# One scale for gate and up, and a new order for the end of the first attention block, in a one-core language-model block

## Chip, core and metric

The kernel runs on one core of one Trainium2 chip. The metric is the device time of one execution in microseconds (us); lower is better. The core's engines are named as in the profile: PE (TensorE: matmuls, with its weight loads as PEld), DVE (VectorE), ACT (ScalarE), POOL (GpSimd) and SP (SyncE, which here only issues DMAs).

## What is computed

The reference takes token ids of shape (2, 1024) with 128 possible values, and gives 2048 rows of 512 numbers. Cut to what matters:

```python
h = rms_norm(rms_norm(emb[x], norm_weight) @ proj.T)            # 2048 rows of 512
a = layernorm(h)
q, k, v = a @ wq, a @ wk, a @ wv      # 32 query heads, 8 key/value heads, 16 wide
y = causal_softmax(q @ k.T / 4) @ v   # each key/value head serves 4 query heads
h = h + y @ wo
b = layernorm(h)
return h + (silu(b @ w_gate.T) * (b @ w_up.T)) @ w_down.T       # hidden width 2048
```

Since h before the attention depends on the token alone, the kernel builds tables over the 128 tokens, and works on rows fetched from them.

## The kernel before

**Blocks and slots.** The 2048 rows are 16 tiles of 128 (`t`), two tiles to a block (`n`, 0 to 7). `phase(n, att, ffn, m)` is called on each engine for n = 0 to 8. It interleaves the attention of block n with the feed-forward part of block m = n - 1 in 24 slots (`s`). Phase 0 has attention alone, and is the stage that the change touches most; the last phase has the feed-forward part alone. The order on each engine is the order in which the code is written, slot by slot, with the places of single steps in tables of slot numbers (`FIRST_SLOTS` for phase 0, `HI_FIRST`, `LOW_FIRST`, `GRAM`, `FILL`). Nothing reorders it. Engines wait for each other by semaphores.

**Attention.** A block has 16 units (`V`), one for a tile and a key/value head. Of unit V = 16n + s, slot s holds on PE `score(V)` and `turn(V+1)` (a transpose of the next queries), on ACT the copy `stack` and the exponential (L516), and on DVE the multiplication with the counts (L835), whose semaphore is `w_rdy`. PE's `values(V)` follows two slots later in phases 0 and 1. After each pair of units DVE takes a reciprocal (L842) and writes a part of `y` (L845); the eighth pair of phase 0 ends the block's attention.

**End of a tile.** For each tile the slot tables place a chain of steps: `yt` (PE transposes y, L1140; ACT copies it as f16 high half, L550; DVE makes the low half, L863), `wo` (PE, 12 products of 512 columns: high by high, high by low and low by high for four chunks, L1148 to L1150), `ln` (DVE: the sum `h1`, L871, and its statistics, L873 to L875), `rs` (DVE: a reciprocal root in eight small dependent steps, L586 to L590), `xhat` (DVE, L881), `xn` (PE transposes, L1155; ACT high half, L559) and `xl` (DVE low half, L885). `tail(t)` is the PSUM bank that these steps share: bank 0 for tile 0, bank 7 for all others. In the text, yt(1) is that step of tile 1.

**Weights of the feed-forward part.** Gate, up and down come as f32 in 24 chunks of 1024 columns, and each is split into an f16 high half by ACT (`split_high`, L482 and L483) and a low half by DVE (`split_low`, L774 and L776). In chunks 0 to 15 the first 512 columns are gate and the others up, each with a scale of its own. The scales come from Gram products, 128 of 128x128 for gate and up (`gate_up_gram`) and 64 for down (L1174, table `GRAM`): DVE takes the diagonals (L738, L739), PE sums them over partitions (L1132), DVE takes the maximum and makes powers of two (`weight_scales`). Chunks 0 to 3 are split in phase 0 and the others in phase 1, one a slot. PE's filler products (L1168, table `FILL`) write results that nobody reads.

**Feed-forward.** `gate_up(m, s)` makes one hidden chunk of 128 in 24 products of 256 columns (L1112 to L1114): gate and up, four chunks each, by high-high, high-low and low-high. The first call, `gate_up(0, 0)`, stands at the head of phase 1. Its wait is

```python
if s == 0:
    pe.wait_ge(xt_lo, m * TPB + TPB)
```

which asks for the low halves of both tiles of the block.

## Time and profile before

| | |
|---|---|
| median of 3 runs | 723.21 us (722.03 to 723.68) |
| profiled execution, its own time | 722.6 us |
| its span, first to last instruction | 720.9 us |
| granted TensorE clock, mean | 0.985 of full speed |
| busy: PE, DVE, ACT, POOL | 693.6, 413.4, 334.1, 295.6 us |
| matmuls | 6399 |

The span is 1.7 us shorter than the execution's own time. The tables over the tokens take the first 45 us, phase 0 runs from there to about 92.8 us, and phase 1 begins with the first gate product at 92.8 us.

### The profile page before, as it was taken

To read this page: it belongs to the slowest core of one execution; us is meant where nothing else is said; L and a number is where in the kernel's file an instruction comes from. 1 tells how busy PE (TensorE), PEld (TensorE's weight loads), DVE (VectorE), ACT (ScalarE), POOL (GpSimd) and SP (SyncE) were. 2 spreads that over 40 slices of the span, in tenths; PEclk is the share of its full clock that TensorE was granted. 3 is DMA by queue.
4 is the path that set the end of the run, shared out by engine and by line. 5 is a ranking of instruction groups with operands and counts; after the bars stand their busy time and mean duration, and the time that the engine had idled before them with its cause. 6 is when DMAs were issued, how large, how long until landed. Compare 5 with 4: busy or idle time off the path is not lost.

```text
span 720.9 us, 16337 instructions
## 1 busy us (share of the span) xinstructions
PE 693.6 (96%) x6399; PEld 530.9 (74%) x6399; DVE 413.4 (57%) x1038; ACT 334.1 (46%) x692; POOL 295.6 (41%) x398
## 2 busy tenths in 40 slices
PE   8459999999999999999999999999999999999998
PEld 5359679974898569965997489856996499847873
DVE  7767789885654456554655465455655365543320
ACT  6426378762565226631665046522674066512320
POOL 5020212241365426752565436642665246611220
PEclk9859999999999999999999999999999999999999
DMA  8759400011000110002000210012000300000000
GB/s 314 307 199 409 145 38 1 2 30 61 33 2 1 61 62 2 2 20 96 7 2 2 70 53 3 1 47 75 2 2 1 107 15 2 1 16 15 2 1 29
DMA packets 10459, 40.37 MB, mean 56 GB/s; under 512 B 1808, under 2 KB 2576, under 8 KB 8592
## 3 DMA queue, kind: packets, MB, share of 16 engines
q1 hardware_dynamic: 6912, 25.44, 9.0%
q0 software_dynamic: 3328, 13.11, 5.8%
q8 instruction: 51, 0.84, 0.5%
q10 hardware_dynamic: 144, 0.79, 0.3%
q14 instruction: 24, 0.20, 0.1%
HBM read 29.89 MB, written 9.44 MB: 55 GB/s over the span
## 4 chain that ended last, share of the span: by engine, by line
PE 89%; DVE 7%; ACT 2%; issue 1%; POOL 1%; DVEq 0%; ACTq 0%; POOLq 0%
PE banks L1112 15%; PE banks L1113 15%; PE banks L1114 15%; PE banks L1203 6%; PE banks L1205 6%; PE banks L1204 6%; PE banks L1066 4%; PE banks L1084 3%; PE banks L1055 2%; PE banks L1148 2%; PE banks L1149 2%; PE banks L1150 2%; PE banks L1046 1%; PE banks L1090 1%; PE banks L1091 1%
## 5 line engine op out<-in xcount | busy, mean ns | idle before, releaser
L1114 PE MATMUL banks<-xnT_and_h,ffn_weights 128*128 128x256 f16 x1024 | 279.0, 272 | 0.0
L1113 PE MATMUL banks<-xnT_and_h,ffn_weights 128*128 128x256 f16 x1024 | 278.9, 272 | 0.0
L1112 PE MATMUL banks<-xnT_and_h,ffn_weights 128*128 128x256 f16 x1024 | 278.8, 272 | 0.1
L375 POOL TENSOR_TENSOR gated_split<-gate_work,gated_split 128x256 f16<-128x256 f32 x128 | 86.7, 677 | 260.6 <-ACT gated_split L520 260.6
L379 POOL TENSOR_TENSOR weights_split<-weights,weights_split 128x512 f16<-128x512 f32 x96 | 111.3, 1160 | 0.0
L1112 PEld LDWEIGHTS banks<-xnT_and_h,ffn_weights 128*128 128x128 f16 x1024 | 101.0, 99 | 11.8 <-DVE xnT_and_h L885 0.6
L1114 PEld LDWEIGHTS banks<-xnT_and_h,ffn_weights 128*128 128x128 f16 x1024 | 100.0, 98 | 11.7
L1113 PEld LDWEIGHTS banks<-xnT_and_h,ffn_weights 128*128 128x128 f16 x1024 | 100.0, 98 | 11.3
L508 ACT ACTIVATE gate_work<-banks,scales 128x256 f32<-128x256 f32 x128 | 60.6, 474 | 99.8 <-PE banks L1114 99.6
L835 DVE SCALAR_TENSOR_TENSOR weights<-weights,counts_T 128x512 f32<-128x512 f32 x128 | 87.8, 686 | 10.9 <-ACT weights L516 10.8
L516 ACT ACTIVATE weights<-banks,scales 128x512 f32<-128x512 f32 x128 | 87.3, 682 | 14.5 <-PE banks L1066 14.5
L801 DVE COPY q_stack<-banks 128x256 f16<-128x256 f16 x96 | 27.8, 290 | 102.8 <-PE banks L1055 102.8
L823 DVE SCALAR_TENSOR_TENSOR gate_work<-gate_work,banks 128x256 f32<-128x256 f32 x128 | 52.9, 414 | 58.9 <-ACT gate_work L508 58.6
L1205 PE MATMUL banks<-ffn_weights,gated_split 128*128 128x512 f16 x224 | 84.9, 379 | 0.0
L1204 PE MATMUL banks<-ffn_weights,gated_split 128*128 128x512 f16 x224 | 84.9, 379 | 0.0
L1203 PE MATMUL banks<-ffn_weights,gated_split 128*128 128x512 f16 x224 | 84.8, 379 | 0.0
L520 ACT ACTIVATE gated_split<-gate_work 128x256 f16<-128x256 f32 x128 | 53.4, 417 | 67.5 <-DVE gate_work L828 67.5
L526 ACT ACTIVATE weights_split<-weights 128x512 f16<-128x512 f32 x96 | 58.9, 614 | 0.0
L828 DVE SCALAR_TENSOR_TENSOR gate_work<-banks,gate_work 128x256 f32<-128x256 f32 x128 | 54.3, 424 | 4.4
L331 POOL DMA_INDIRECT token_rows<-token_table,indices x16 | 15.7, 983 | 92.5 <-DVE xnT_and_h L871 86.9
L559 ACT ACTIVATE xnT_and_h<-banks 128x512 f16<-128x512 f32 x16 | 9.6, 597 | 81.0 <-PE banks L1155 80.5
L1066 PE MATMUL banks<-q_stack,k_stack_even 128*128 128x128 f16 x256 | 42.7, 220 | 1.0 <-ACT q_stack L491 1.0
(241 smaller groups left out, 1065.1 us busy)
## 6 DMA issues: line engine op xcount, KB each, us to landing
ffn_weights<-in_ffn_w SPq DMA_DIRECT2D x12, 1024.0 KB, 10.2
out_rows_dram<-ffn_weights SPq DMA_DIRECT2D x16, 256.0 KB, 2.0
xnT_and_h<-in_wqkv SPq DMA_DIRECT2D x1, 1536.0 KB, 8.9
local_table<-gated_split SPq DMA_DIRECT2D x2, 640.0 KB, 4.5
local_table<-xnT_and_h SPq DMA_DIRECT2D x2, 640.0 KB, 5.7
gated_split<-in_projT SPq DMA_DIRECT2D x4, 256.0 KB, 4.4
ffn_weights<-in_wo SPq DMA_DIRECT2D x1, 1024.0 KB, 10.9
token_table<-weights_split ACTq DMA_DIRECT2D x1, 768.0 KB, 5.6
```

Source lines behind the costliest of these rows:

```text
L375: g.tensor_tensor(gtl[:, j, :], g2[j % 2], gth[:, j, :], ALU.subtract).then_inc(gt_lo, 1)
L379: g.tensor_tensor(WTl[V % RING], E[V % RING][:, :], WTh[V % RING], ALU.subtract).then_inc(wt_lo, 1)
L508: a.activation(th[j % 2], f_bank[j % 3][:, 0:BLK], ACT.Tanh, scale=c_tanh).then_inc(th_rdy, 1)
L516: a.activation(E[V % RING][:, :], b_S[V % 2], ACT.Exp, scale=c_exp).then_inc(exp_done, 1)
L835: v.scalar_tensor_tensor(w, w, SEEN_MAX, cT[:, t * P:(t + 1) * P].unsqueeze(1).broadcast_to([P, REP, P]), ALU.min, ALU.mult).then_inc(w_rd ...
L1066: last = t.matmul(b_S[V % 2][:, (2 * j + a) * P:(2 * j + a + 1) * P], (KstA, KstB)[a][:, gr * P:(gr + 1) * P], Qst[:, r * 256 + j * P:r * ...
L1112: t.matmul(o, wh, xTh[m % 2][:, c, :], start=c == 0, stop=False)
L1113: t.matmul(o, wh, xTl[m % 2][:, c, :], start=False, stop=False)
L1114: last = t.matmul(o, wl, xTh[m % 2][:, c, :], start=False, stop=c == DC - 1)
L1203: t.matmul(o, hh, dn_w(j, 0), start=j == 0, stop=False)
L1204: t.matmul(o, hh, dn_w(j, 1), start=False, stop=False)
L1205: last = t.matmul(o, hl, dn_w(j, 0), start=False, stop=j == HC - 1)
```

## The change

Gate and up get one common scale: the Gram products of both accumulate in one bank, one diagonal is taken and summed, and each chunk is split by one operation of 1024 columns on ACT and one on DVE. Chunks 0 to 3 are split in other slots of phase 0. The down Gram products, 64 in four slots from 16 on, become 64 in three slots from 17 on, behind the last `values`. `wo` takes its high halves first and waits for the low half of y ahead of the last four products only; for tile 1 it writes bank 4 (`b_S[0]`). `h1` gets a slot entry of its own, ahead of `ln`. The copy that signalled `y_rdy` in phase 0 (L849) goes, and yt waits on `pv_ev`. In all gate and up chunks the four high-by-low-activation products of gate, and of up, stand behind the other eight, and the first gate product of a block waits for the high halves of both tiles and the low half of the first. The diff, cut to its core:

```diff
-FIRST_SLOTS = dict(yt=(11, 18), wo=(13, 19), ln=(16, 20), rs=(17, 20), xhat=(19, 20), xn=(20, 21), xl=(21, 21), ...
+FIRST_SLOTS = dict(yt=(11, 18), wo=(13, 19), h1=(16, 20), ln=(17, 20), rs=(19, 20), xhat=(19, 20), xn=(20, 21), xl=(21, 21), ...
-HI_FIRST = {16: 0, 17: 1, 20: 2, 21: 3}
-LOW_FIRST = {19: (0,), 21: (1,), 22: (2,), 23: (3,)}
+HI_FIRST = {13: 0, 16: 1, 17: 2, 21: 3}
+LOW_FIRST = {13: (0,), 21: (1,), 22: (2,), 23: (3,)}
-GRAM = {16: (0, 12), 17: (12, 24), 18: (24, 44), 19: (44, 64)}
+GRAM = {17: (0, 18), 18: (18, 34), 19: (34, 64)}
...
+        def wo_bank(t):
+            return b_S[0] if t == 1 else tail(t)
...
-                a.activation(half(i, 0)[:, 0:512], raw(i)[:, 0:512], ACT.Copy, scale=s_g if i < 16 else s_d)
-                a.activation(half(i, 0)[:, 512:1024], raw(i)[:, 512:1024], ACT.Copy,
-                             scale=s_u if i < 16 else s_d).then_inc(split_hi, 1)
+                a.activation(half(i, 0), raw(i), ACT.Copy, scale=s_gu if i < 16 else s_d).then_inc(split_hi, 1)
...
-                v.tensor_tensor(t_gu_diag[:, 0:P], f_bank[2][:, 0:P], ident[:, :], ALU.mult)
-                v.tensor_tensor(t_gu_diag[:, P:2 * P], b_tail[:, 0:P], ident[:, :], ALU.mult).then_inc(tab["gu_diag"], 1)
+                v.tensor_tensor(t_gu_diag, f_bank[2][:, 0:P], ident[:, :], ALU.mult).then_inc(tab["gu_diag"], 1)
...
-                        if i == 3:
-                            dve.wait_ge(pv_ev, pair + 1)
-                            v.tensor_scalar(st[:, 25:26], rden[k][:, 0:1], 1.0, None, ALU.mult).then_inc(y_rdy, 1)
...
             def gate_up(m, s):
                 i = m * HC + s
                 if s == 0:
-                    pe.wait_ge(xt_lo, m * TPB + TPB)
+                    pe.wait_ge(xt_hi, m * TPB + TPB)
+                    pe.wait_ge(xt_lo, m * TPB + 1)
...
                     for c in range(DC):
                         wh, wl = (gu_w(s, up, c, h) for h in (0, 1))
                         t.matmul(o, wh, xTh[m % 2][:, c, :], start=c == 0, stop=False)
-                        t.matmul(o, wh, xTl[m % 2][:, c, :], start=False, stop=False)
-                        last = t.matmul(o, wl, xTh[m % 2][:, c, :], start=False, stop=c == DC - 1)
+                        t.matmul(o, wl, xTh[m % 2][:, c, :], start=False, stop=False)
+                    if s == 0 and up == 0:
+                        pe.wait_ge(xt_lo, m * TPB + TPB)
+                    for c in range(DC):
+                        last = t.matmul(o, gu_w(s, up, c, 0), xTl[m % 2][:, c, :], start=False, stop=c == DC - 1)
...
                         if att and s == at["wo"][k]:
-                            pe.wait_ge(yt_lo, tl + 1)
+                            if tl == 1:
+                                pe.wait_ge(yt_hi, tl + 1)
+                            else:
+                                pe.wait_ge(yt_lo, tl + 1)
```

**PE, slots 16 to 19 of phase 0.** In the kernel before, `ffn_weights` rows are the down Gram products, the `v_full_one` rows are values(14) and values(15), and L1140 is yt(1); the first `wo_split` row opens wo(1):

```order
L1084 MATMUL banks<-v_full_one,weights 128x17 [waits w_ready,pv_evacuated]
L1084 MATMUL banks<-v_full_one,weights 128x17 x3
L1174 MATMUL banks<-ffn_weights 128x128 [waits ffn_pair8_in]
L1174 MATMUL banks<-ffn_weights 128x128 x11
L1084 MATMUL banks<-v_full_one,weights 128x17 [waits w_ready]
L1084 MATMUL banks<-v_full_one,weights 128x17 x3
...
L1140 MATMUL banks<-ident,xnT_and_h 128x128 [waits y_ready]
L1140 MATMUL banks<-ident,xnT_and_h 128x128 x3
...
L1148 MATMUL banks<-wo_split,yT_split 128x512 [waits yT_lo]
```

The same place in the changed kernel, where L1082 is `values`, L1186 the down Gram products, L1145 yt(1), and L1156, L1157 and L1162 are wo(1):

```order
L1082 MATMUL banks<-v_full_one,weights 128x17 [waits w_ready,pv_evacuated]
L1082 MATMUL banks<-v_full_one,weights 128x17 x3
L1082 MATMUL banks<-v_full_one,weights 128x17 [waits w_ready]
L1082 MATMUL banks<-v_full_one,weights 128x17 x3
L1186 MATMUL banks<-ffn_weights 128x128 [waits ffn_pair8_in]
...
L1145 MATMUL banks<-ident,xnT_and_h 128x128 [waits pv_evacuated]
L1145 MATMUL banks<-ident,xnT_and_h 128x128 x3
...
L1156 MATMUL banks<-wo_split,yT_split 128x512 [waits yT_hi]
...
L1162 MATMUL banks<-wo_split,yT_split 128x512 [waits yT_lo]
```

values(15) now stands directly behind values(14), ahead of all Gram products. Between it and yt(1) stand 18 of them where there were 12, between yt(1) and wo(1) 16 where there were 20, and behind wo(1) 30 where there were 20. wo(1) waits for the high half of y first.

**DVE, slots 16 to 20 of phase 0.** In the kernel before, from h1(0) to h1(1) (both L871), with the pair of the last values (L842, L845), the eight steps of rs(0) (L586 to L590, of which two stand here), yt(1)'s low half (L863), xhat(0) (L881) and the split of chunk 0 (L774, L776):

```order
L875 TENSOR_SCALAR ln_stats<-ln_stats 128x1 [waits vector_step]
L842 RECIPROCAL rden<-banks 128x8 [waits pv_ready,vector_step]
L845 TENSOR_TENSOR xnT_and_h<-banks,rden 128x128 [waits rden_ready]
L849 TENSOR_SCALAR ln_stats<-rden 128x1 [waits pv_evacuated]
L586 TENSOR_SCALAR ln_stats<-ln_stats 128x1
L587 TENSOR_SCALAR ln_stats<-ln_stats 128x1 [waits vector_step]
...
L863 TENSOR_TENSOR yT_split<-banks,yT_split 128x512 [waits yT_hi,vector_step]
L881 TENSOR_SCALAR xn<-xnT_and_h,ln_stats 128x512
L774 SCALAR_TENSOR_TENSOR ffn_weights<-ffn_weights,scales 128x512 [waits split_hi]
L776 SCALAR_TENSOR_TENSOR ffn_weights<-ffn_weights,scales 128x512
L871 SCALAR_TENSOR_TENSOR xnT_and_h<-banks,scales,token_rows 128x512 [waits wo_ready]
```

In the changed kernel, from the pair of the last values (L841, L844) to h1(1) (L868), with the low half of y at L860:

```order
L841 RECIPROCAL rden<-banks 128x8 [waits pv_ready]
L844 TENSOR_TENSOR xnT_and_h<-banks,rden 128x128 [waits rden_ready]
L871 BN_STATS ln_stats<-xnT_and_h 128x6 [waits h1_ready]
L872 BN_AGGR ln_stats<-ln_stats 128x2 [waits vector_step]
L873 TENSOR_SCALAR ln_stats<-ln_stats 128x1 [waits vector_step]
L860 TENSOR_TENSOR yT_split<-banks,yT_split 128x512 [waits yT_hi,vector_step]
L591 TENSOR_SCALAR ln_stats<-ln_stats 128x1
...
L879 TENSOR_SCALAR xn<-xnT_and_h,ln_stats 128x512 [waits vector_step]
L868 SCALAR_TENSOR_TENSOR xnT_and_h<-banks,scales,token_rows 128x512 [waits wo_ready]
```

The last pair moved ahead of tile 0's statistics, the low half of y ahead of rs(0), and the split of chunk 0 out of this stretch.

**DVE, slots 13 to 15.** In the changed kernel the split of chunk 0 (L777) stands behind the scale (L751) and ahead of the multiplications of units 14 and 15 (L834), for which values(14) and values(15) wait; ACT's half of it stands likewise ahead of the stack and the exponentials of these units:

```order
L750 TENSOR_SCALAR scales<-scales 128x1
L751 TENSOR_SCALAR scales<-scales 128x1
L777 SCALAR_TENSOR_TENSOR ffn_weights<-ffn_weights,scales 128x1024 [waits split_hi,tab_gu_scaled]
L834 SCALAR_TENSOR_TENSOR weights<-weights,counts_T 128x512 [waits exp_done] x2
L841 RECIPROCAL rden<-banks 128x8 [waits pv_ready]
```

Before, nothing stood between the scale and the two multiplications.

## Rows read from the trace of the kernel before

**Rows 1.** The page's chain that ended last, shares of the span by engine:

```profile
PE 89%; DVE 7%; ACT 2%; issue 1%; POOL 1%; DVEq 0%; ACTq 0%; POOLq 0%
```

**Rows 2.** Busy us (x count) of PE, PEld, DVE, ACT, POOL; granted clock; DMA:

```profile
100.00:160.00 60.00, 60.00 (x571) 53.42 (x569) 54.30 (x99) 46.17 (x99) 17.71 (x25) 1.00 0.01 2
```

**Rows 3.** Timeline of PE: start, us, operation, idle before it:

```profile
71.32 0.70 PE L1132 MATMUL banks<-gate_work,xnT_and_h 128*128 128x256 f32 x2
...
77.60 0.96 PE L1084 MATMUL banks<-v_full_one,weights 128*128 128x17 f32 x8
...
79.09 1.01 PE L1084 MATMUL banks<-v_full_one,weights 128*128 128x17 f32 x8
79.95 0.85 PE L1174 MATMUL banks<-ffn_weights 128*128 128x128 bf16 x12
81.35 0.66 PE L1140 MATMUL banks<-ident,xnT_and_h 128*128 128x128 f32 x4 [0.54 <-DVE ln_stats L849]
...
83.68 0.39 PE L1148 MATMUL banks<-wo_split,yT_split 128*128 128x512 f16 x1 [0.53 <-DVE yT_split L863]
...
86.28 1.31 PE L1174 MATMUL banks<-ffn_weights 128*128 128x128 bf16 x20
...
90.73 0.66 PE L1155 MATMUL banks<-ident,xn 128*128 128x128 f32 x4 [0.97 <-DVE xn L881]
91.22 0.39 PE L1165 MATMUL banks<-gate_work,xnT_and_h 128*128 128x128 f32 x2
91.44 1.24 PE L1168 MATMUL banks<-counts_T,ident 128*128 128x512 f16 x5
92.80 0.28 PE L1112 MATMUL banks<-xnT_and_h,ffn_weights 128*128 128x256 f16 x1
...
93.03 0.27 PE L1114 MATMUL banks<-xnT_and_h,ffn_weights 128*128 128x256 f16 x1
```

**Rows 4.** Timeline of DVE:

```profile
70.98 0.28 DVE L739 TENSOR_TENSOR gate_work<-banks,ident 128x128 f32<-128x128 f32 x1
...
74.03 0.20 DVE L747 TENSOR_SCALAR scales<-scales 128x1 f32<-128x1 f32 x1
...
77.22 0.69 DVE L835 SCALAR_TENSOR_TENSOR weights<-weights,counts_T 128x512 f32<-128x512 f32 x1 [0.48 <-ACT weights L516]
...
80.57 0.21 DVE L842 RECIPROCAL rden<-banks 128x8 f32<-128x8 f32 x1 [0.40 <-DVE ln_stats L875]
...
81.21 0.14 DVE L586 TENSOR_SCALAR ln_stats<-ln_stats 128x1 int32<-128x1 int32 x1
...
82.93 0.69 DVE L863 TENSOR_TENSOR yT_split<-banks,yT_split 128x512 f16<-128x512 f32 x1
83.54 0.54 DVE L881 TENSOR_SCALAR xn<-xnT_and_h,ln_stats 128x512 f32<-128x512 f32 x1
83.99 0.74 DVE L774 SCALAR_TENSOR_TENSOR ffn_weights<-ffn_weights,scales 128x512 f16<-128x512 f32 x1
...
86.48 0.75 DVE L871 SCALAR_TENSOR_TENSOR xnT_and_h<-banks,scales,token_rows 128x512 f32<-128x512 f32 x1 [1.08 <-PE banks L1150]
...
92.05 0.69 DVE L885 SCALAR_TENSOR_TENSOR xnT_and_h<-banks,xnT_and_h 128x512 f16<-128x512 f32 x1 [0.58 <-ACT xnT_and_h L559]
```

**Rows 5.** Timeline of ACT:

```profile
75.26 0.68 ACT L516 ACTIVATE weights<-banks,scales 128x512 f32<-128x512 f32 x1
...
82.12 0.60 ACT L550 ACTIVATE yT_split<-banks 128x512 f16<-128x512 f32 x1 [2.48 <-PE banks L1140]
```

**Rows 6.** One line's instructions each: duration ns min/median/max, first and last start:

```profile
L472 ACT ACTIVATE wo_split<-ffn_weights,scales x2: 1144/1148/1151, 50.9 to 52.8; 128x1024 f16<-128x1024 f32 x2
...
L733 DVE SCALAR_TENSOR_TENSOR wo_split<-ffn_weights,scales,wo_split x2: 1279/1280/1280, 59.1 to 66.9; 128x1024 f16<-128x1024 f32 x2
...
L774 DVE SCALAR_TENSOR_TENSOR ffn_weights<-ffn_weights,scales x16: 741/1118/1235, 84.0 to 141.0; 128x512 f16<-128x512 f32 x16
```

**Rows 7.** The page's costliest groups: busy, mean ns | idle before:

```profile
L1114 PE MATMUL banks<-xnT_and_h,ffn_weights 128*128 128x256 f16 x1024 | 279.0, 272 | 0.0
```

More of the change, by code:

```diff
@@ L238, in col @@
             return sc[:, i:i + n]
-        s_q, s_k, s_v, s_wo, s_g, s_u, s_d = (col(8 + i) for i in range(7))
+        s_q, s_k, s_v, s_wo, s_gu, s_d = (col(8 + i) for i in range(6))
         r_q, r_k, r_v = (col(16 + i) for i in range(3))
@@ L863, in phase @@
                             v.tensor_tensor(yT[:, D:2 * D], tail(t), yT[:, 0:D], ALU.subtract).then_inc(yt_lo, 1)
-                        if att and s == at["ln"][k]:
+                        if att and s == at["h1"][k]:
                             dve.wait_ge(wo_rdy, t + 1)
@@ L870, in phase @@
                                 dve.wait_ge(fin_rdy, t - 3)
-                            v.scalar_tensor_tensor(h1[t % 4], tail(t), c_vo, h0g[k], ALU.mult, ALU.add).then_inc(h1_rdy, 1)
+                            v.scalar_tensor_tensor(h1[t % 4], wo_bank(t), c_vo, h0g[k], ALU.mult, ALU.add).then_inc(h1_rdy, 1)
+                        if att and s == at["ln"][k]:
                             dve.wait_ge(h1_rdy, t + 1)
@@ L894, in phase @@
                         stack((n + 1) * UPB)
+                    if n == 0 and s == GU_SCALE_SLOT:
+                        weight_scales()
                     if n == 0:
@@ L903, in phase @@
                         place_max(1)
-                    if n == 0 and s == GU_SCALE_SLOT:
-                        weight_scales()
                     if n == 0 and s == WO_SCALE_SLOT:
@@ L1045, in gate_up_gram @@
                     w = raw_pair(i).bitcast(BF16)[:, o:o + 2 * P - 1:2]
-                    last = t.matmul((f_bank[2], b_tail)[m][:, 0:P], w, w, start=u == 8 * m, stop=u == 112 + 8 * m + 7)
+                    last = t.matmul(f_bank[2][:, 0:P], w, w, start=u == 0, stop=u == 127)
                 return last
@@ L1131, in phase @@
                         pe.wait_ge(tab["gu_diag"], 1)
-                        t.matmul(b_tail[:, P:3 * P], ones32, t_gu_diag, start=True, stop=True).then_inc(tab["gu_sum"], 1)
+                        t.matmul(b_tail[:, P:2 * P], ones32, t_gu_diag, start=True, stop=True).then_inc(tab["gu_sum"], 1)
                     for k in range(TPB):
@@ L1146, in phase @@
                             for c in range(DC):
-                                yh, yl = (yT[:, i * D + c * P:i * D + (c + 1) * P] for i in (0, 1))
-                                t.matmul(tail(tl), yh, Woh[:, c, :], start=c == 0, stop=False)
-                                t.matmul(tail(tl), yh, Wol[:, c, :], start=False, stop=False)
-                                last = t.matmul(tail(tl), yl, Woh[:, c, :], start=False, stop=c == DC - 1)
+                                yh = yT[:, c * P:(c + 1) * P]
+                                t.matmul(wo_bank(tl), yh, Woh[:, c, :], start=c == 0, stop=False)
+                                t.matmul(wo_bank(tl), yh, Wol[:, c, :], start=False, stop=False)
+                            if tl == 1:
+                                pe.wait_ge(yt_lo, tl + 1)
+                            for c in range(DC):
+                                yl = yT[:, D + c * P:D + (c + 1) * P]
+                                last = t.matmul(wo_bank(tl), yl, Woh[:, c, :], start=False, stop=c == DC - 1)
                             last.then_inc(wo_rdy, 1)
```

38 lines of the change are left out of this document (20 added, 18 removed).

## Prediction

> **What bounds the kernel now.** I read the chain of waits first. PE holds 89% of it and DVE 7% [rows 1], so time can be won only where PE waits, or where it does work that nobody needs. The view by stretches says where that is: from 100 to 160 us PE is busy for 60.00 of 60 us at a granted clock of 1.00 [rows 2]. So from phase 1 on a start that comes earlier should move everything behind it by as much. What is left is the end of phase 0, and there I read the timelines of PE, DVE and ACT beside each other.
>
> The chain there runs as follows. values(15) starts at 79.09 us on PE and its pair is taken up by DVE at 80.57 [rows 3, 4]. PE meanwhile does 12 Gram products, and then idles 0.54 us until yt(1) at 81.35 [rows 3]. DVE does the eight steps of rs(0) from 81.21 to 82.93, and only then the low half of y, though ACT's high half, started at 82.12 and 0.60 long, was done at 82.72 [rows 4, 5]. wo(1) waits for that and starts at 83.68 [rows 3]. h1(1) starts at 86.48 [rows 4]. From there a fixed chain on DVE (statistics, root, xhat) leads to the transposes xn(1) at 90.73, ACT's high half and DVE's low half, which starts at 92.05 and takes 0.69, and the first gate product at 92.80 [rows 3, 4]. DVE's split of chunk 0, at 83.99 [rows 4], stands in this stretch but ahead of a wait for PE, which costs h1(1) nothing.
>
> **The change, part by part.** I lay the changed order out with the durations of the rows.
>
> *Scale of gate and up.* PE's sum at 71.32 [rows 3] waits for the second diagonal, which starts on DVE at 70.98 and is 0.28 long [rows 4]. Without it the sum starts between nothing and 0.28 earlier; I take 0.15. The sum over 256 columns runs 0.70 to its end, one over 128 columns 0.39 (L1165) [rows 3]: 0.31 less. Together 0.46. wo(0) and all that PE has in order behind it can be that much earlier: values(14), which started at 77.60 without a wait [rows 3], could start at 77.14.
>
> *Split of chunk 0 in slot 13.* The last step of the scale starts at 74.03 [rows 4]; with a maximum over half the columns I put it at 73.9, and ACT starts at about 74.14. A split of 1024 columns takes 1.15 on ACT [rows 6]: until 75.29. Behind it on ACT wait the stack for score(15) and the exponential of unit 14, which started at 75.26 before [rows 5] and now at about 75.47, ending at 76.15. DVE starts its half of the split at 75.34 and is free 1.20 later (1.28 long, with the usual overlap of 0.08) [rows 6]: 76.54. Behind it waits the multiplication of unit 14, done now at 77.23, and that of unit 15, done at 77.84, as against 77.91 before (77.22 + 0.69) [rows 4]. So values(14) starts at 77.28, not at 77.14: it gains 0.32. Bounds: 0.46 if the wait is shorter, and nothing or a loss of 0.3 if the handovers between ACT and DVE take 0.3 to 0.6 more. I stay near the rows, since GpSimd is idle then: the split's longest times, 1235 ns as against 741 [rows 6], are from phase 1.
>
> *values(15) ahead of the Gram products.* It follows values(14) by 0.86 (79.09 to 79.95) [rows 3]: 78.14, 0.95 earlier. Of this 0.63 is the first Gram share, 12 products of 0.057 each (0.85 less a last one of 0.22, over 11) [rows 3].
>
> The Trainium skill ("TensorE: Matmul & The Clock Gate", Back-to-back issue gap) gives about 81 ns for each product of 128 columns in a stream with its weight loads, where the row has 57. By its figure, an estimate, the 18 and 16 products that now stand before and behind yt(1) would take 0.8 us more than by the row, of which about 0.6 would reach the chain. The row is of these very products, and I keep to it.
>
> *yt(1).* DVE took up the pair 1.48 after values(15) started (80.57 - 79.09) and yt(1) started 0.78 later; I take 0.19 off for the copy L849, since small DVE steps that wait for each other follow at about that (eight of them in the 1.72 of rs(0)) [rows 4]: 0.59. So yt(1) starts 2.07 after values(15): 80.21, and 18 Gram products (0.86 + 1.03 = 1.89) hide under this. It gains 1.14. Of the 1.48, 0.4 is idle time that I can't put to a cause; if it goes, the products bound it, and the gain is 0.18 more.
>
> *Low half of y, and wo(1).* Let Y be the start of yt(1). ACT's high half starts 0.77 after it (82.12 - 81.35), and ends at Y + 1.37 [rows 3, 5]. On PE the transposes (0.49) and 16 Gram products (0.92) end at Y + 1.41, so wo(1) starts at Y + 1.42. DVE now waits with the low half ahead of rs(0), so rs(0), xhat(0) and h1(1) are queued behind that wait; it ends at Y + 2.11, while PE has high products until Y + 3.15. wo(1) ends 2.60 after its start (83.68 to 86.28) [rows 3], and its signal takes 0.20: Y + 4.22. On DVE the low half holds the engine 0.61, rs(0) 1.72 (81.21 to 82.93) and xhat(0) 0.45 (83.54 to 83.99) [rows 4]: free at Y + 4.20. Both meet, and h1(1) starts at Y + 4.22, where it was Y + 5.13. It gains 0.91 more, together 2.05. The next thing late is DVE's own queue: nothing more is to be had here by a faster PE. Bank 4 for wo(1) costs nothing by itself, since DVE reads bank 7 meanwhile.
>
> *Down to the first gate product.* From h1(1) to xn(1) nothing changes (4.25). The 30 Gram products behind wo(1) take 1.7 and the 8 fillers 1.7, which end before xn(1) at 88.68. Then PE has 0.49 of transposes, 0.22, and five fillers, which end 1.08 after 91.44 before, that is 1.79 after xn(1). ACT's high half is done 1.3 after xn(1), just ahead of 92.05. So the fillers bound the first gate product, at 1.79 where the low half gave 2.07: 0.28 more. Tile 1's low half, done 2.0 after xn(1), is asked for only behind eight products of about 0.11 each (92.80 to 93.03 for two) [rows 3], at 2.67.
>
> *Everything else.* The merged splits in phase 1 save about 0.12 on DVE and 0.17 on ACT in each chunk, but PE waits for neither there [rows 2]: worth nothing. POOL's fetches hang on h1 and move with it. The sum is 0.32 + 0.63 + 0.19 + 0.91 + 0.28 = 2.33 us. The profiled execution took 722.6 by its own time, and should take 720.3; from the median of 723.21, which is 0.6 above it, I come to **720.9**.
>
> **The rivals.**
>
> *It gives less, 0 to 1.4 us (about 722.4).* The split of chunk 0 stands in slot 13 ahead of the last two units. Each us by which the multiplication of unit 14 is later than 77.23 is a us on values(14) and all behind. If ACT and DVE together take 0.9 more, through a collision as in phase 1 (up to 0.5 on one split [rows 6]) and longer handovers, the gain falls to 1.4. Against it: ACT's and DVE's times for exactly these shapes are in the rows, and POOL has no work then.
>
> The Trainium skill ("Perfetto Trace Analysis", Optimizing Scalar/DVE Operations) says that where these engines aren't saturated but hold up others, breaking instructions up may let work be done sooner. By that rule the merged operations would be the wrong way here. The trace speaks against it in this place, since both halves were signalled together before.
>
> *It gets slower (from 723.7 on).* All gate and up products change their order: 3072 of them, with a mean of 272 ns in each of the three lines, of which one is shown [rows 7]. If two products in a row on one moving operand, or weights that change each time, cost 1 ns more each, that is 3.1 us, and 723.21 - 2.3 + 3.1 = 724.0. From 0.76 ns on it takes the whole gain. Against it: the three kinds stand in three different neighbourhoods now (same weights as before, same moving operand, or neither), and their three rows agree within 0.2 us in 279 [rows 7]. It is the only part that touches the bound stage.
>
> *The gain is lost again.* If phase 1 were held by DVE or ACT with PE only seeming busy, an earlier start would be eaten up, and the time stay at 723. DVE is busy 54.30 of 60 us there, so it is near [rows 2]; but PE shows no gap, and DVE's load falls.
>
> **How the numbers follow.** The case of the sum, gain between 1.4 and 2.8, has 0.76: 720.4 to 721.8. More than that has 0.04. Less, 0 to 1.4, has 0.13, the lost gain counted in. Slower through the products' rate or something unseen has 0.07. The runs before spread by 1.7, so a median may be off by some tenths; that widens the range to 719.8 to 722.3. A change of 0.2%, 1.4 us, is about what can be told from none: faster by more 0.79, within it 0.14, slower 0.07.
>
> **What would show it.** values(14) at about 77.3 and values(15) at 78.1 directly behind it; yt(1) near 80.2; wo(1) near 81.6 with DVE's low half of y running under it; h1(1) near 84.4, directly behind xhat(0) on DVE; the first gate product near 90.5, right behind the fillers. From there the gate products must keep following at about 0.11, and PE without gaps. The prediction is wrong if the first gate product moved by 2.3 and the end didn't, if values(14) waits for DVE beyond 77.6, or if the mean of the gate products is no longer 272 ns.

## The result, and the profile after

The changed kernel takes 721.12 us (median of 20 runs, 720.29 to 722.72) and the kernel before, on the same chip, 722.89. One of its 20 runs was in a slower state, at 739.27; such runs count in no ratio here, nor in any median from here on, and without it the kernel before has 722.77. The ratio is 0.9979, 95% interval 0.9972 to 0.9986: faster by 0.21%. The profiled execution took 720.69 by its own time, with a span of 718.9 and a mean granted clock of 0.986. The page of the changed kernel (busy times, chain, gate and up products):

```profile
PE 693.0 (96%) x6399; PEld 530.6 (74%) x6399; DVE 409.4 (57%) x1019; ACT 329.7 (46%) x668; POOL 297.1 (41%) x398
...
PE 89%; DVE 6%; ACT 2%; issue 1%; POOL 1%; DVEq 0%; ACTq 0%; POOLq 0%
...
L1112 PE MATMUL banks<-xnT_and_h,ffn_weights 128*128 128x256 f16 x1024 | 237.3, 272 | 0.0
L1111 PE MATMUL banks<-xnT_and_h,ffn_weights 128*128 128x256 f16 x1024 | 237.2, 272 | 0.0
...
L1116 PE MATMUL banks<-xnT_and_h,ffn_weights 128*128 128x256 f16 x1024 | 153.6, 273 | 0.0
```

The chain is PE's as before [rows 1], with 6% instead of 7% for DVE. The three lines of gate and up products have means of 272, 272 and 273 ns where the row of before had 272 [rows 7]; their busy sums can't be compared, since the view joins products that follow each other on one line. From 100 to 160 us PE is full, as before [rows 2], and DVE is down from 54.30 to 51.84 us:

```profile
100.00:160.00 60.00, 60.00 (x561) 52.64 (x559) 51.84 (x92) 42.76 (x81) 20.89 (x25) 1.00 0.04 11
```

The timeline of PE at the end of phase 0 (start, us, operation, idle before), which answers to [rows 3]:

```profile
70.90 0.49 PE L1134 MATMUL banks<-gate_work,xnT_and_h 128*128 128x128 f32 x2
71.22 0.38 PE L1156 MATMUL banks<-wo_split,yT_split 128*128 128x512 f16 x1
...
77.19 1.93 PE L1082 MATMUL banks<-v_full_one,weights 128*128 128x17 f32 x16
78.97 1.20 PE L1186 MATMUL banks<-ffn_weights 128*128 128x128 bf16 x18
80.00 0.60 PE L1145 MATMUL banks<-ident,xnT_and_h 128*128 128x128 f32 x4
80.44 1.08 PE L1186 MATMUL banks<-ffn_weights 128*128 128x128 bf16 x16
81.72 0.39 PE L1156 MATMUL banks<-wo_split,yT_split 128*128 128x512 f16 x1 [0.20 <-ACT yT_split L555]
...
84.32 1.88 PE L1186 MATMUL banks<-ffn_weights 128*128 128x128 bf16 x30
...
88.79 0.66 PE L1167 MATMUL banks<-ident,xn 128*128 128x128 f32 x4 [0.42 <-DVE xn L879]
...
89.51 1.24 PE L1180 MATMUL banks<-counts_T,ident 128*128 128x512 f16 x5
90.58 0.27 PE L1111 MATMUL banks<-xnT_and_h,ffn_weights 128*128 128x256 f16 x1
90.69 0.27 PE L1112 MATMUL banks<-xnT_and_h,ffn_weights 128*128 128x256 f16 x1
```

The same stretch on DVE, which answers to [rows 4]:

```profile
75.15 1.28 DVE L777 SCALAR_TENSOR_TENSOR ffn_weights<-ffn_weights,scales 128x1024 f16<-128x1024 f32 x1 [1.35 <-ACT ffn_weights L488]
76.36 1.29 DVE L834 SCALAR_TENSOR_TENSOR weights<-weights,counts_T 128x512 f32<-128x512 f32 x2
...
79.15 0.21 DVE L841 RECIPROCAL rden<-banks 128x8 f32<-128x8 f32 x1 [0.39 <-PE banks L1082]
...
81.77 0.69 DVE L860 TENSOR_TENSOR yT_split<-banks,yT_split 128x512 f16<-128x512 f32 x1 [1.07 <-ACT yT_split L555]
...
84.09 0.55 DVE L879 TENSOR_SCALAR xn<-xnT_and_h,ln_stats 128x512 f32<-128x512 f32 x1
84.55 0.75 DVE L868 SCALAR_TENSOR_TENSOR xnT_and_h<-banks,scales,token_rows 128x512 f32<-128x512 f32 x1
...
90.11 0.69 DVE L883 SCALAR_TENSOR_TENSOR xnT_and_h<-banks,xnT_and_h 128x512 f16<-128x512 f32 x1 [0.58 <-ACT xnT_and_h L564]
```

And on ACT [rows 5]:

```profile
73.89 1.15 ACT L488 ACTIVATE ffn_weights<-ffn_weights,scales 128x1024 f16<-128x1024 f32 x1 [2.78 <-DVE scales L751]
...
81.07 0.60 ACT L555 ACTIVATE yT_split<-banks 128x512 f16<-128x512 f32 x1 [2.44 <-PE banks L1145]
```

The first gate product is at 90.58 where it was at 92.80. But executions differ by up to 1.7 us in the time at which they reach phase 0's second half, and they do so for one and the same kernel too (69.95 and 71.25). So I measure from values(11), ahead of wo(0): at 70.18 before, 69.95 here, and at 69.8 to 71.5 over all profiles of this study. In the eight profiles in which PE is busy throughout from 49 to 55 us it goes with the granted clock there: 69.95 at 0.86, down to 71.52 at 0.71. The other six have 0.82 to 1.00 there and idle for 0.04 to 0.93 us, and are as late as 71.25, so the clock alone doesn't account for it. From values(11) to each step:

| us after values(11) | before | forecast | changed |
|---|---|---|---|
| values(14) | 7.42 | 7.10 | 7.24 |
| yt(1) | 11.17 | 10.03 | 10.05 |
| wo(1) | 13.50 | 11.4 | 11.77 |
| h1(1) | 16.30 | 14.25 | 14.60 |
| xn(1) | 20.55 | 18.50 | 18.84 |
| first gate product | 22.62 | 20.29 | 20.63 |
| from there to the end of the span | 628.1 | 628.1 | 628.3 |

The stretch is 1.99 shorter, values(11) was 0.23 earlier by chance, and 0.2 is given back behind the first gate product: together the 2.0 between the spans of 720.9 and 718.9.

### The profile page after: what moved, and what is told of

It is laid out like the page before. It is cut to its first block, busy times and chain, and to the rows that moved or that the text cites. A ratio compares the mean times of both kernels' runs of the same rounds, so it can differ in the third digit from the quotient of the medians.

```text
span 718.9 us, 16283 instructions
## 1 busy us (share of the span) xinstructions
PE 693.0 (96%) x6399; PEld 530.6 (74%) x6399; DVE 409.4 (57%) x1019; ACT 329.7 (46%) x668; POOL 297.1 (41%) x398
## 4 chain that ended last, share of the span: by engine, by line
PE 89%; DVE 6%; ACT 2%; issue 1%; POOL 1%; DVEq 0%; ACTq 0%; POOLq 0%
PE banks L1111 15%; PE banks L1116 15%; PE banks L1112 15%; PE banks L1215 6%; PE banks L1217 6%; PE banks L1216 6%; PE banks L1064 4%; PE banks L1082 4%; PE banks L1053 2%; PE banks L1156 2%; PE banks L1162 2%; PE banks L1157 2%; PE banks L1044 1%; PE banks L1088 1%; PE banks L1089 1%; PE banks L1145 1%
## 5 line engine op out<-in xcount | busy, mean ns | idle before, releaser
L1112 PE MATMUL banks<-xnT_and_h,ffn_weights 128*128 128x256 f16 x1024 | 237.3, 272 | 0.0
L1111 PE MATMUL banks<-xnT_and_h,ffn_weights 128*128 128x256 f16 x1024 | 237.2, 272 | 0.0
L1116 PE MATMUL banks<-xnT_and_h,ffn_weights 128*128 128x256 f16 x1024 | 153.6, 273 | 0.0
L1111 PEld LDWEIGHTS banks<-xnT_and_h,ffn_weights 128*128 128x128 f16 x1024 | 100.9, 99 | 11.4
L834 DVE SCALAR_TENSOR_TENSOR weights<-weights,counts_T 128x512 f32<-128x512 f32 x128 | 87.5, 684 | 9.1 <-ACT weights L520 8.8
```

The costliest lines, as they stand in the source:

```text
L834: v.scalar_tensor_tensor(w, w, SEEN_MAX, cT[:, t * P:(t + 1) * P].unsqueeze(1).broadcast_to([P, REP, P]), ALU.min, ALU.mult).then_inc(w_rd ...
L1111: t.matmul(o, wh, xTh[m % 2][:, c, :], start=c == 0, stop=False)
L1112: t.matmul(o, wl, xTh[m % 2][:, c, :], start=False, stop=False)
L1116: last = t.matmul(o, gu_w(s, up, c, 0), xTl[m % 2][:, c, :], start=False, stop=c == DC - 1)
```

## Experiments

The theory of the prediction was: each part shortens the stretch by its own wait, and nothing else moves. Its rivals were the split in slot 13, the rate of the reordered products, and an early start that phase 1 eats up. Of each kernel one execution was profiled. Where a step is given from values(11), its clock was 1.00 there unless the text says otherwise.

**The order of the products.** *u_gate* is the changed kernel with the products and the wait of the first gate product as before:

```diff
-                    pe.wait_ge(xt_hi, m * TPB + TPB)
-                    pe.wait_ge(xt_lo, m * TPB + 1)
+                    pe.wait_ge(xt_lo, m * TPB + TPB)
...
-                        t.matmul(o, wl, xTh[m % 2][:, c, :], start=False, stop=False)
...
+                        t.matmul(o, wh, xTl[m % 2][:, c, :], start=False, stop=False)
+                        last = t.matmul(o, wl, xTh[m % 2][:, c, :], start=False, stop=c == DC - 1)
```

> The changed kernel with the gate and up products in the order of before, and the first gate product waiting for both low halves again. Theory (the change works through the chain at the end of phase 0): the first gate product comes 0.28 us later after xn(1) (2.07 as before, 1.79 with the change), nothing else moves, so 0.3 us slower than the changed kernel and 1.2 to 1.5 faster than the kernel before. Rival (the order of the products changes PE's rate, and gave or took part of the gain in 3072 products): the time from the first gate product to the end of the span differs from the changed kernel's 628.3 us by over 0.5 us.

*gate_alone* makes only this edit, the other way round, on the kernel before.

> The kernel before with the new order of the gate and up products and the new waits of the first gate product alone. Theory: the first gate product starts 1.79 us after xn(1), where the low half made it 2.07: 0.28 us faster than before, 0.1 to 0.4 in the times. Rival (the order changes PE's rate): a difference of over 0.5 us either way, in the stretch behind the first gate product.

*u_gate* took 720.64 (ratio 0.9975, 0.9966 to 0.9985), *gate_alone* 722.76 (1.0001, 0.9992 to 1.0010). From the first gate product to the end, *gate_alone* needs 628.0 and *u_gate* 628.4, against 628.1 and 628.3 with the other order: 3072 reordered products cost 0.1 at most, and the rival that made it slower is ruled out. Timeline of PE in *gate_alone*:

```profile
90.77 0.66 PE L1159 MATMUL banks<-ident,xn 128*128 128x128 f32 x4 [0.97 <-DVE xn L881]
...
91.48 1.24 PE L1172 MATMUL banks<-counts_T,ident 128*128 128x512 f16 x5
92.56 0.27 PE L1113 MATMUL banks<-xnT_and_h,ffn_weights 128*128 128x256 f16 x1
```

The first gate product comes 1.79 after xn(1), behind the fillers, where it was 2.07: the 0.28 of the sum to the digit. It is too little to show in the times: *gate_alone* was no faster than the kernel before, and *u_gate*, forecast 0.3 slower than the changed kernel, has a median 0.5 lower, with intervals that overlap. *u_gate* has 2.07 again, yet its stretch, 20.50, is shorter than the changed kernel's 20.63. The reason is another step: ACT takes up yt(1) 0.64 after it starts (80.59 to 81.23), where the changed kernel's profile has 1.07. PE and ACT in *u_gate*:

```profile
80.59 0.60 PE L1141 MATMUL banks<-ident,xnT_and_h 128*128 128x128 f32 x4
```

```profile
81.23 0.60 ACT L555 ACTIVATE yT_split<-banks 128x512 f16<-128x512 f32 x1 [2.01 <-PE banks L1141]
```

With *u_gate*'s hand-over the changed kernel would stand at 20.50 - 0.28 = 20.22, and the next three, which have the short one too (0.64 to 0.69), are measured against that.

**The slots of the splits.** *u_slots* is the changed kernel with the splits where they were:

```diff
-HI_FIRST = {13: 0, 16: 1, 17: 2, 21: 3}
-LOW_FIRST = {13: (0,), 21: (1,), 22: (2,), 23: (3,)}
+HI_FIRST = {16: 0, 17: 1, 20: 2, 21: 3}
+LOW_FIRST = {19: (0,), 21: (1,), 22: (2,), 23: (3,)}
```

> The changed kernel with chunks 0 to 3 split in the slots of before (ACT in 16, 17, 20, 21, DVE in 19, 21, 22, 23). Theory (DVE's queue and PE's wo(1) reach h1(1) at the same time in the changed kernel): DVE's split of chunk 0, 1.20 us, now stands between xhat(0) and h1(1) and makes h1(1) 1.2 later, of which about 0.1 to 0.3 comes back because values(14) no longer waits for DVE; 0.9 to 1.1 us slower than the changed kernel, so 0.4 to 1.0 faster than before. Rival (DVE has slack there, only PE's order counts): no slower than the changed kernel, rather 0.2 faster.

It took 722.25 (0.9997, 0.9988 to 1.0006), and its stretch is 21.46. In the times nearly all of the gain is gone, where 0.4 to 1.0 had been expected to stay. By the stretch more stays: it is 1.16 shorter than before, and 0.95 is left with what is given back behind it. That lies just outside the interval, which ends at 0.87, and the runs don't show where the rest of the time goes. Timeline of its DVE:

```profile
84.20 0.55 DVE L879 TENSOR_SCALAR xn<-xnT_and_h,ln_stats 128x512 f32<-128x512 f32 x1
84.66 1.28 DVE L777 SCALAR_TENSOR_TENSOR ffn_weights<-ffn_weights,scales 128x1024 f16<-128x1024 f32 x1
85.86 0.74 DVE L868 SCALAR_TENSOR_TENSOR xnT_and_h<-banks,scales,token_rows 128x512 f32<-128x512 f32 x1
```

wo(1) had ended on PE at 84.13, but h1(1) stands behind the split of chunk 0 and starts at 85.86. The same split cost nothing before, since DVE waited 1.08 for PE there [rows 4]. Now h1(1) starts 5.68 after yt(1), where *u_gate* has 4.15: 1.53 more. Of this 0.29 comes back ahead of yt(1), which leaves the stretch 1.24 longer (21.46 - 20.22): values(14) comes 7.01 after values(11), against 7.24, so in slot 13 the split takes 0.23 from it.

**The place of the Gram products.** *u_gram* puts them back:

```diff
-GRAM = {17: (0, 18), 18: (18, 34), 19: (34, 64)}
+GRAM = {16: (0, 12), 17: (12, 24), 18: (24, 44), 19: (44, 64)}
```

> The changed kernel with the 64 down Gram products placed as before (12, 12, 20, 20 in slots 16 to 19). Theory: values(15) starts 0.69 us later behind 12 products, yt(1) 0.6 later, and the 20 products between yt(1) and wo(1) end 0.2 after ACT's high half, so the first gate product is 0.8 us later than in the changed kernel. Rival (the Gram products are hidden under the handovers to DVE and ACT): the first gate product moves by less than 0.3 us.

721.71 (0.9987, 0.9978 to 0.9996); the stretch 20.92. values(15) is 8.81 after values(11), yt(1) 10.45, which is 0.40 later than in the changed kernel. wo(1) comes 1.64 after yt(1), behind 20 Gram products where there were 16, and the stretch is 0.70 longer than 20.22.

**wo(1) by high halves first.** *u_wo* only makes wo(1) wait for the low half again:

```diff
                             if tl == 1:
-                                pe.wait_ge(yt_hi, tl + 1)
+                                pe.wait_ge(yt_lo, tl + 1)
```

> The changed kernel with wo(1) waiting for the low half of y ahead of its first product, the order of its products kept. Theory: wo(1) starts after DVE's low half, 0.7 us later, and h1(1) and the first gate product are 0.7 us later. Rival (DVE's queue in front of h1(1) is what counts, since it ends at the same time as wo(1)): under 0.2 us later.

721.41 (0.9985, 0.9976 to 0.9994). Timeline of its PE:

```profile
81.05 0.60 PE L1145 MATMUL banks<-ident,xnT_and_h 128*128 128x128 f32 x4
...
83.14 0.39 PE L1156 MATMUL banks<-wo_split,yT_split 128*128 128x512 f16 x1 [0.57 <-DVE yT_split L860]
```

wo(1) comes 2.09 after yt(1), against 1.36 in *u_gate* with the same hand-over, and the stretch is 20.98: 0.76 longer than 20.22. *wo_alone* brings the order of wo, bank 4 and the wait for the high half to the kernel before:

```diff
+                            if tl == 1:
+                                pe.wait_ge(yt_hi, tl + 1)
+                            else:
+                                pe.wait_ge(yt_lo, tl + 1)
...
-                                last = t.matmul(tail(tl), yl, Woh[:, c, :], start=False, stop=c == DC - 1)
...
+                            if tl == 1:
+                                pe.wait_ge(yt_lo, tl + 1)
+                            for c in range(DC):
+                                yl = yT[:, D + c * P:D + (c + 1) * P]
+                                last = t.matmul(wo_bank(tl), yl, Woh[:, c, :], start=False, stop=c == DC - 1)
```

> The kernel before with the new order of wo's products, wo(1) in bank 4 and waiting for the high half of y alone at its head. Theory: wo(1) starts 0.9 us earlier, at the end of ACT's high half, since the low half is late behind rs(0) on DVE and is there before it is asked for; h1(1) and the first gate product come 0.9 earlier, as DVE is done with its split of chunk 0 at 85.3 us: 0.6 to 1.0 faster than the kernel before. Rival (the three moves only pay together): under 0.3.

721.98 (0.9986, 0.9977 to 0.9995); stretch 21.92, 0.70 less than before. wo(1) starts 1.64 after yt(1), right behind 20 Gram products, and h1(1) 4.43 after it, where it was 5.13. It is the largest of the three parts that were made alone, and the only one of them that shows in the times.

**The common scale.** *scale_alone* is the kernel before with one scale, one diagonal and merged splits, in their old slots:

```diff
-                    last = t.matmul((f_bank[2], b_tail)[m][:, 0:P], w, w, start=u == 8 * m, stop=u == 112 + 8 * m + 7)
+                    last = t.matmul(f_bank[2][:, 0:P], w, w, start=u == 0, stop=u == 127)
...
-                v.tensor_tensor(t_gu_diag[:, P:2 * P], b_tail[:, 0:P], ident[:, :], ALU.mult).then_inc(tab["gu_diag"], 1)
```

> The kernel before with the common scale and the merged split operations alone, all slots as before. Theory: the sum over 128 columns and the one diagonal let wo(0) start about 0.5 us earlier on PE, and all up to values(14) with it, so the first gate product comes 0.4 to 0.5 us earlier; the merged splits give nothing, except where DVE's split of chunk 0 stands, under a wait for PE. Rival (the units behind it are held by ACT and DVE, not by PE's order): under 0.15 us; second rival (the merged splits relieve DVE in phase 1, which was the bound there): over 1 us, in the stretch behind the first gate product.

722.44 (0.9994, 0.9986 to 1.0003); stretch 22.12, 0.50 less. values(14) is at 7.01 and values(15) at 8.52, 0.39 earlier than before. The rest is in two hand-overs: DVE takes up the last pair 0.05 after it is free and values(15) has ended, where it took 0.40 before, which makes yt(1) another 0.22 earlier, and ACT is later behind yt(1), which takes 0.11 back. Nothing is given back behind the first gate product (628.0).

**Fewer fillers.** After the change the fillers bound the first gate product, which the kernels so far only inferred. *fill2* takes three of them away:

```diff
-FILL = {14: 2, 15: 2, 20: 8, 21: 5}
+FILL = {14: 2, 15: 2, 20: 8, 21: 2}
```

> The changed kernel with 2 fillers in slot 21 where there were 5. Theory: these fillers bound the first gate product, which then starts when ACT's high half is done, 1.32 us after xn(1) and not 1.79: 0.45 us faster than the changed kernel, 2.0 to 2.4 faster than before; the low half of tile 1 is in time behind eight products. Rival: the start is given back in phase 1, where chunk 1 to 3 and the next block's units wait for DVE, and the time stays; or the granted clock falls with less work on PE, and phase 1 gets slower by several us.

720.08 (0.9966, 0.9953 to 0.9979), stretch 20.24. The first gate product is at 90.99, 1.35 after xn(1) instead of 1.79, and now it is ACT that holds it, whose high half ends at 90.93 (timeline of ACT in *fill2*):

```profile
81.92 0.60 ACT L555 ACTIVATE yT_split<-banks 128x512 f16<-128x512 f32 x1 [2.50 <-PE banks L1145]
...
90.33 0.60 ACT L564 ACTIVATE xnT_and_h<-banks 128x512 f16<-128x512 f32 x1 [2.21 <-PE banks L1167]
```

**Three ways to have more.** *split_moved* is *fill2* with the splits in slots where they disturb neither values(14) nor h1(1):

```diff
-HI_FIRST = {13: 0, 16: 1, 17: 2, 21: 3}
-LOW_FIRST = {13: (0,), 21: (1,), 22: (2,), 23: (3,)}
+HI_FIRST = {15: 0, 16: 1, 20: 2, 21: 3}
+LOW_FIRST = {17: (0,), 21: (1,), 22: (2,), 23: (3,)}
```

> The kernel best with the fillers of slots 14 and 15 back (2 fillers in slot 21, chunk 0 split in ACT's slot 15 and DVE's slot 17). Theory (best lost its gain to the granted clock, 0.68 of full speed from 80 to 85 us, for want of those fillers): the clock stays at 1.00 there, values(14) starts behind PE's own order 0.2 us earlier than in the changed kernel, and the first gate product 20.0 us after values(11) as against 20.24 in fill2; 2.2 to 2.8 us faster than the kernel before. Rival (the clock falls because of the other 3 fillers or by chance): below 0.95 again in that stretch. Second rival: DVE's split in slot 17 makes the low half of y late, and the first gate product comes later than in fill2.

720.58 (0.9970, 0.9958 to 0.9981), stretch 20.29 where 20.0 was expected. values(14) is at 7.01, as it should be. But the timeline of DVE shows what takes the place of the wait:

```profile
80.53 1.28 DVE L777 SCALAR_TENSOR_TENSOR ffn_weights<-ffn_weights,scales 128x1024 f16<-128x1024 f32 x1 [0.30 <-DVE ln_stats L873]
81.73 0.68 DVE L860 TENSOR_TENSOR yT_split<-banks,yT_split 128x512 f16<-128x512 f32 x1
...
84.04 0.55 DVE L879 TENSOR_SCALAR xn<-xnT_and_h,ln_stats 128x512 f32<-128x512 f32 x1
84.50 0.75 DVE L868 SCALAR_TENSOR_TENSOR xnT_and_h<-banks,scales,token_rows 128x512 f32<-128x512 f32 x1
```

The split holds DVE until the low half of y at 81.73, 0.58 after ACT's high half ended (80.55 + 0.60); rs(0) and xhat(0) follow, and h1(1) starts at 84.50 although wo(1) had ended at 83.80, so that it is 3.30 behind the start of wo(1), against 2.79 in *u_gate*. What values(14) wins is lost in DVE's queue. *root_early* therefore has rs(0) in slot 18 and the low half of chunk 0 in slot 19:

```diff
-FIRST_SLOTS = dict(yt=(11, 18), wo=(13, 19), h1=(16, 20), ln=(17, 20), rs=(19, 20), xhat=(19, 20), ...
+FIRST_SLOTS = dict(yt=(11, 18), wo=(13, 19), h1=(16, 20), ln=(17, 20), rs=(18, 20), xhat=(19, 20), ...
...
-LOW_FIRST = {17: (0,), 21: (1,), 22: (2,), 23: (3,)}
+LOW_FIRST = {19: (0,), 21: (1,), 22: (2,), 23: (3,)}
```

> The kernel split_moved with rs(0) in slot 18, ahead of the low half of y, and DVE's split of chunk 0 in slot 19, behind xhat(0). In split_moved DVE was free for h1(1) 0.50 us after wo(1) and its signal were done. Theory: rs(0) fills DVE's wait for the high half of y, the low half comes just before wo(1) asks for it, xhat(0) and the split end 0.2 us after wo(1), and the first gate product comes 20.0 to 20.1 us after values(11) as against 20.29; 0.2 to 0.3 faster than split_moved, 2.2 to 2.9 faster than the kernel before. Rival: the low half of y comes too late behind rs(0), PE waits inside wo(1), and nothing is won.

720.60 (0.9965, 0.9951 to 0.9979), the same again. Its profiled execution, 721.67, lost clock (0.50 from 80 to 82 us), so its stretch of 21.08 can't be set against 20.29. In it h1(1) is 2.79 behind the start of wo(1) again, and DVE idles 0.96 ahead of it; but the low clock had made wo(1) late and so gave DVE time, and what the edit is worth at full clock stays open. *best*, made ahead of these two, has *split_moved*'s tables and leaves out the fillers of slots 14 and 15 too:

```diff
-FILL = {14: 2, 15: 2, 20: 8, 21: 2}
+FILL = {20: 8, 21: 2}
```

> The changed kernel with 2 fillers in slot 21, none in slots 14 and 15, and chunk 0 split behind the last exponential (ACT in slot 15, DVE in slot 17 behind tile 0's statistics, where it idles 1.07 us; ACT's chunk 2 back in slot 20). Theory: the last two units are held by nothing but their own chain, values(15) starts 0.9 to 1.1 us earlier than in the changed kernel, DVE's split hides in the wait for the high half of y, and with the fillers' 0.45 the first gate product comes 1.2 to 1.6 us earlier; 2.8 to 3.4 faster than before. Rival (the split in slot 13 costs nothing and the fillers hide under ACT's and DVE's handovers): only the 0.45 of fill2. Second rival: the granted clock falls with fewer fillers, and it is slower.

It took 721.28 (0.9979, 0.9970 to 0.9989), 1.4 less than before where 2.8 to 3.4 was expected: no better than the changed kernel, and 0.70 above *split_moved*, though the two intervals overlap. Its clock fell. Windows of *best* (us, busy and count of PE, PEld, DVE, ACT, POOL; granted clock; DMA):

```profile
78.00:80.00 2.00, 2.00 (x22) 2.00 (x22) 1.71 (x5) 1.76 (x2) 0.20 (x1) 0.94 0.06 16
80.00:82.00 2.00, 2.00 (x18) 2.00 (x17) 1.61 (x5) 0.00 (x0) 1.69 (x2) 0.50 0.36 55
82.00:84.00 2.00, 2.00 (x20) 1.72 (x20) 1.78 (x4) 0.60 (x1) 1.42 (x1) 0.71 0.85 334
```

The stretch is 20.44, 0.15 longer than in *split_moved*, although PE had four products less to do and ACT took up yt(1) as soon as it ended. All ten of its runs that count have a mean clock of 0.981 to 0.983, which no run of *split_moved* has (0.986 to 0.988). In the profile the fall takes what the missing fillers gave and 0.15 more; whether the rest of the 0.70 is real, and how it comes about, isn't shown.

**The changed kernel again.** *after_again* has no edit. It asks whether the hand-over to ACT, and this clock, belong to the kernel or to the execution.

> The changed kernel once more, unchanged. From the start of values(11) to the first gate product it had 20.63 us. In its first profile ACT took up the transposes of yt(1) 1.07 us after they started, in three of its variants 0.64, in one 1.13. Theory: this differs by execution and not by kernel, so that the stretch is 20.2 to 20.3 in an execution with 0.64, where the 16 Gram products bound wo(1), and 20.6 in one with 1.07. Rival: it belongs to the kernel, and is 1.07 again. Time against the kernel before: 0.9965 to 0.9985.

721.34 (0.9977, 0.9967 to 0.9987). Its profiled execution was its slowest, 723.15, and shows the clock of *best* without any edit (windows, columns as above):

```profile
78.00:80.00 2.00, 1.94 (x16) 1.54 (x14) 1.97 (x5) 1.93 (x2) 0.00 (x0) 1.00 0.04 14
80.00:82.00 2.00, 2.00 (x24) 2.00 (x24) 1.50 (x6) 0.00 (x0) 1.36 (x2) 0.70 0.12 23
82.00:84.00 2.00, 2.00 (x18) 1.93 (x17) 0.51 (x1) 0.60 (x1) 1.46 (x2) 0.50 0.89 270
84.00:86.00 2.00, 2.00 (x14) 1.05 (x12) 1.72 (x10) 0.00 (x0) 0.00 (x0) 0.94 0.32 121
```

In the changed kernel's first profile all these windows have 1.00. The stretch is 21.83 here, 1.2 longer. Its rows of yt(1) and of ACT's high half also bear on the other question, PE first:

```profile
81.70 1.05 PE L1145 MATMUL banks<-ident,xnT_and_h 128*128 128x128 f32 x4
```

```profile
82.79 0.60 ACT L555 ACTIVATE yT_split<-banks 128x512 f16<-128x512 f32 x1 [2.87 <-PE banks L1145]
```

ACT starts 1.09 after yt(1), as it did in the first profile (1.07). But the four transposes take 1.05 at this clock, not 0.60: ACT starts 0.04 after they end (82.75), where in the first profile it started 0.47 after (81.07 - 80.60). So by its end ACT took them up at once here. Since the transposes themselves were slow, this alone doesn't settle it: from their start the distance is the same as in the first profile. The stronger sign is in kernels whose programs are the changed kernel's up to this step: *u_gate* and *u_wo* have 0.04 from end to start, *fill2* has 0.53, all at a clock of 1.00. Counted from the end, the hand-over took 0.03 to 0.04 in *after_again*, *u_gate*, *u_slots*, *u_gram*, *u_wo*, *best* and *root_early*, 0.10 to 0.13 in the kernel before, *gate_alone* and *wo_alone*, and 0.33 to 0.53 in *scale_alone*, *split_moved*, *fill2* and the changed kernel's first profile.

## Why the prediction was right

*The place and the mechanism.* The gain is where the prediction put it, between values(11) and the first gate product, and it passes through the bound stage: 1.99 us of the stretch, less 0.2 given back behind it, go with 1.65 us of the medians (722.77 to 721.12; 2.1 from the 723.21 shown). So the gain was forecast 0.7 too high, and that 720.9 comes within 0.2 of the median is partly luck, since the 723.21 of three runs that it starts from was 0.4 above the median of the 19. Alone on the kernel before, three parts give 0.50 (scale, of which 0.39 up to values(15)), 0.70 (wo) and 0.28 (gate) us of the stretch; that they add up was not tried.

*Scale and split in slot 13, forecast 0.32, measured 0.18.* The scale by itself gives 0.41 (7.42 to 7.01, in four kernels) of 0.46. The split takes back 0.23 of it, where I had put 0.14. DVE's order ran as worked out: ACT's split at 3.94 after values(11) (forecast 3.96), DVE's at 5.20 (5.16), the multiplications at 6.41 (6.36). From the end of the first of them to values(14) went 0.14, where I had allowed 0.05. This was the first rival's mechanism, at a tenth of its price.

*values(15) and yt(1), forecast 0.82 together, measured 0.94.* values(14) and (15) are one row of 16, and yt(1) starts 2.81 after values(14) began, right behind the 18 Gram products. The 0.4 that the prediction couldn't put to a cause is gone. Before, by the profile, values(15) had ended at 80.10 (79.09 + 1.01) and DVE was free at 80.17, yet it took up the pair at 80.57 [rows 3, 4]. Now values(15) ends at 79.12 (77.19 + 1.93) and DVE starts at 79.15; its 0.39 of idle time there is plain waiting for PE. The pair is written by 79.69, ahead of the end of the Gram products, so these bound yt(1), as the prediction said they would if the 0.4 went. It stands in *gate_alone* and *wo_alone* as before (0.41), and in no kernel with the common scale (0.03 to 0.05); why, no run shows. yt(1) starts 1.03 after the first of the 18, which makes 57 ns each. The 81 ns of the Trainium skill ("TensorE: Matmul & The Clock Gate", Back-to-back issue gap) don't hold for these products.

*wo(1) and h1(1), forecast 0.91, measured 0.58.* This is the term that was mis-sized. The step was "ACT's high half starts 0.77 after it"; it was 1.07 here (80.00 to 81.07). PE had its 16 products done and idled 0.20 for ACT, so wo(1) starts at Y + 1.72, not Y + 1.42, and h1(1) at Y + 4.55, not Y + 4.22. The rest of the step holds: DVE becomes free for h1(1) (xhat(0) at 84.09, 0.45 long) just when PE is done (84.32 + 0.20), as foreseen. The long hand-over is one of this execution and not of the kernel, since *u_gate* and *u_wo*, with the same program up to this step, don't have it. Of the four profiles of this program with the clock at 1.00, two have 0.64 and two have 1.07 and 1.13 (*fill2*); 0.77 is neither, and which of them was profiled is luck. In *u_gate*, where it took 0.64, h1(1) is at Y + 4.15, and by the 20.22 worked out there the changed kernel's stretch is then 2.40 shorter than before, for a forecast of 2.33.

*Down to the first gate product, forecast 0.28, measured 0.28*: 1.79 after xn(1), shown by *gate_alone* and, through the fillers, by *fill2*.

*Everything else at nothing.* 0.2 is given back: from the first gate product on 628.3 to 628.4 pass in the changed kernel and in all eight built on it, 628.0 to 628.1 in the kernel before and the three built on that. PE waits 1.9 us instead of 1.6 for ACT's copies of the values there. I have not found what does it; the scale, the order of the products or the order of wo alone don't, and it stays when the slots of the splits or of the Gram products are as before.

*What is not settled.* Why ACT takes up finished transposes 0.04 us after their end in one execution and 0.3 to 0.5 after it in another, and how often. The difference is 0.4 us on the path. In *u_gate*, with the short hand-over, the Gram products stand behind yt(1) as in the changed kernel's first profile, POOL's fetch starts 0.29 after yt(1) against 0.28, and the DMA queues' next burst comes within the same 0.2 us, so neither is enough to make it. Also open is the 0.4 between values(15) and DVE in the kernel before.

*Is there a better version?* *fill2*, *split_moved* and *root_early* have ratios of 0.9966, 0.9970 and 0.9965, each with its interval overlapping the changed kernel's. Three fewer fillers are worth 0.44 in the profile (1.79 to 1.35), and they had the long hand-over in *fill2* and *split_moved* at that. Whether the times are really lower than the changed kernel's, and which of the three is best, these runs can't tell.

## What to carry to other kernels

When several engines' queues meet at one step within tenths of a microsecond, an edit on one of them is worth only what the next queue leaves: here the same split, 1.28 us when it is one operation, cost nothing, 0.2 or 1.5 us by the slot in which it stood. Measure such edits from the last step ahead of them in the trace, since the executions differ by more at that step than the edit is worth, and price a hand-over between engines from several executions, not from one row. Taking out filler products pays only where they are last to end; others may be what keeps the clock up.

## What the runs showed of the hardware

The granted clock fell for 3 to 4 us at about 79 to 84 us in some executions: 0.70, 0.50 and 0.94 in the windows of *after_again*, 0.94, 0.50 and 0.71 in *best*, 0.93, 0.50 and 0.72 in *root_early*. 0.50 is the lower level, 1.2 GHz. PE was busy for 2.00 of 2 us in each of these windows. Ahead of the fall PE did the f32 products of 17 columns of units 14 and 15 back to back, in *best* those of unit 13 with them, and the clock rose again just ahead of wo(1) in *best* and *root_early*, and with it in *after_again*. The fall isn't explained by this, since the changed kernel's first profile has the same products in the same order and no fall. How often it comes only the mean clock of each run can tell, and that not surely: it was 0.983 and 0.981 in the profiled runs of *after_again* and *best*, but 0.986 in that of *root_early*, no lower than without a fall. A mean of 0.981 to 0.983 is found in 1 run of 20 of the changed kernel, 1 of 9 of *after_again*, 1 of 11 of *u_gram*, none of the kernel before, and all ten of *best* that count. What *best* lacks is four products of 512 columns, two behind unit 12 and two behind unit 13. That these fillers hold the clock is argued from this one kernel; *split_moved*, which differs from *best* by them alone, had 1.00 throughout, but *root_early* and *after_again* have them and fell. In the changed kernel a fall costs at least 1.2 us of the stretch (21.83 against 20.63, where the latter had the long hand-over).

Also new to me was the hand-over: with the same program up to this step, ACT started 0.04 us after the end of PE's transposes in *u_gate* and 0.47 after it in the changed kernel's first profile, with nothing else on ACT by the trace (it idled 2.01 and 2.44 us ahead of it).
